# Moving the count of target edges from a graph kernel's second sort into its first, and both spreads of node terms to the start of the second

## The reference

```python
xl = x @ W_lin + b_lin
s_i = xl @ W_att[:hc]
s_j = xl @ W_att[hc:]
alpha = s_i[row] + s_j[col] + b_att
alpha = jnp.where(alpha >= 0, alpha, 0.2 * alpha)
amax = jax.ops.segment_max(alpha, row, num_segments=n)
alpha = jnp.exp(alpha - amax[row])
asum = jax.ops.segment_sum(alpha, row, num_segments=n)
alpha = alpha / (asum[row] + 1e-16)
xh = xl.reshape(n, H, C)
msg = alpha[:, :, None] * xh[row]
out = jax.ops.segment_sum(msg, col, num_segments=n)
```

## Time and profile before

| what | value |
| --- | --- |
| runs | 7012.77, 7015.36 and 7035.64 us |
| the profiled execution | its span is 8156.2 us; no other time of it is given |
| GpSimd busy | 5142.3 us, 63% |
| VectorE busy | 4030.1 us, 49% |
| first sort, block `sa` | 0 to 352 us of the span |
| second sort, block `sd` | 352.6 to 1737 us |
| source softmax, block `st` | 1737 to 1913 us |

### The profile page before, as it was taken

The page is one execution under the profiler, slowest core; times in us unless marked ns, Lnnn a source line. Parts: engine busy times, 40 slices in busy tenths (PEclk is TensorE's granted clock), DMA queues, the critical chain, the costliest instruction groups (busy, mean ns, idle before and its releaser), DMA issues. The chain is left out here.

```text
span 8156.2 us, 28050 instructions
## 1 busy us (share of the span) xinstructions
PE 1077.7 (13%) x4502; PEld 708.5 (9%) x4502; DVE 4030.1 (49%) x8039; ACT 763.0 (9%) x1695; POOL 5142.3 (63%) x4956
## 2 busy tenths in 40 slices
PE   6301022440000000000005565000000001000000
PEld 5200012430000000000003222000000001000000
DVE  8970259673444333333324666667533334336445
ACT  0020012220000000000003333000000003000002
POOL 0277720227777766777764666666777775767774
PEclk9999997775555555555557888555555555555555
DMA  2250000022433333333323677432433331324332
GB/s 49 108 223 2 2 1 0 9 49 63 105 97 97 97 85 101 100 93 93 93 75 118 245 250 252 126 105 70 112 95 93 93 95 44 82 82 122 97 103 60
DMA packets 556796, 772.01 MB, mean 95 GB/s; under 512 B 122155, under 2 KB 433249, under 8 KB 537033
## 3 DMA queue, kind: packets, MB, share of 16 engines
q0 software_dynamic: 159120, 283.64, 14.5%
q1 hardware_dynamic: 379284, 375.57, 14.5%
q10 hardware_dynamic: 18210, 111.02, 3.5%
HBM read 357.68 MB, written 412.16 MB: 94 GB/s over the span
## 5 line engine op out<-in xcount | busy, mean ns | idle before, releaser
L2475 POOL DMA_INDIRECT l2s_krow<-table_k,l2s_idx x784 | 780.9, 996 | 410.5 <-issue 245.8
L929 POOL DMA_INDIRECT l2z_rows<-proj,l2z_idx x784 | 848.6, 1082 | 255.2 <-issue 242.7
L929 POOL DMA_INDIRECT l1z_rows<-table,l1z_idx x784 | 823.4, 1050 | 282.1 <-issue 249.2
L929 POOL DMA_INDIRECT l0z_rows<-table,l0z_idx x784 | 832.3, 1062 | 257.6 <-issue 247.2
L778 POOL DMA_INDIRECT l3z_rows<-table,l3z_idx x784 | 806.0, 1028 | 273.9 <-issue 237.8
L1918 POOL DMA_INDIRECT first_sj<-scores,first_atdst x544 | 559.1, 1028 | 182.2 <-issue 182.2
L2412 DVE SCALAR_TENSOR_TENSOR l2s_qrow<-l2s_qrow,g_dokeep,l2s_zrow 128x82 f32<-128x82 f32 x1568 | 369.3, 300 | 200.6 <-DVE l2s_qrow L2412 138.7
L2430 PE MATMUL l2s_bank<-l2o_wr,l2s_fed 128*128 128x512 f32 x800 | 415.9, 680 | 296.0 <-ACT l2s_fed L2454 171.7
L962 DVE TENSOR_TENSOR l1z_msg<-l1z_rows,l1z_factors 128x1024 f32<-128x1024 f32 (+1 forms) x50 | 60.0, 1200 | 647.4 <-DMA l1z_rows<-table,l1z_idx 633.3
L754 DVE SCALAR_TENSOR_TENSOR l3z_acc<-l3z_acc,l3z_xx,l3z_msg 128x128 f32<-128x128 f32 x784 | 277.8, 354 | 171.8 <-DVE l3z_acc L754 91.5
L962 DVE TENSOR_TENSOR l2z_msg<-l2z_rows,l2z_factors 128x1024 f32<-128x1024 f32 (+1 forms) x50 | 60.0, 1200 | 599.6 <-DMA l2z_rows<-proj,l2z_idx 599.2
(11 more groups left out here) (583 smaller groups left out, 5129.6 us busy)
## 6 DMA issues: line engine op xcount, KB each, us to landing
proj<-l2s_proj ACTq DMA_DIRECT2D x100, 1024.0 KB
spread_q<-prep_zero SPq DMA_DIRECT2D x98, 656.0 KB
l2s_zrow<-spread_q SPq DMA_DIRECT2D x98, 656.0 KB
prefix<-l0z_acc SPq DMA_DIRECT2D x196, 256.0 KB
prefix<-l1z_acc SPq DMA_DIRECT2D x196, 256.0 KB
prefix<-l2z_acc SPq DMA_DIRECT2D x196, 256.0 KB
prefix<-l3z_acc SPq DMA_DIRECT2D x48, 1040.0 KB
l0z_rows<-table,l0z_idx POOLq DMA_INDIRECT x784
```

The lines of the kernel that those rows point to most:

```text
L929: nc.gpsimd.indirect_dma_start(out=rows[:, k % RING, c * (hi - lo) + u, :], out_offset=None, in_=table, in_offset=bass.IndirectOffsetOnAxi ...
L2475: nc.gpsimd.indirect_dma_start(out=krow[:, h, u, :], out_offset=None, in_=g.table_k, in_offset=bass.IndirectOffsetOnAxis(ap=idx[:, h, u:u ...
```

## The change

Four things are moved, and nothing is computed that was not computed before. (1) Both tallies are in the first sort: at each of its 14 turns VectorE offers the batches of the sources and then those of the targets, each kind with a ring of its own, and TensorE counts them in the same order. (2) The positions and node rows of both directions are computed at the end of the first sort, between the last count and the wait for the sorted keys. (3) GpSimd begins the second block with both spreads, 100 indirect DMAs, and fetches the 544 columns of scores behind them; the wait on `placed` is gone, and so is the spread in `st`. (4) The turns of the second sort hold transposes and copies alone.

```diff
--- before.py
+++ after.py
@@ -360,7 +360,7 @@
     chain(v.tensor_scalar(key, key, sign, None, ALU.mult))
 
 
-def sort_by_source(nc, g, a, wide, keys, rows, sjn, raw, count_src, src_s, at_dst):
+def sort_by_source(nc, g, a, wide, keys, rows, sjn, raw, counts, starts, orders, src_s, at_dst):
@@ -382,7 +382,10 @@
         cleared, zeroed, counted = s.sem("cleared"), s.sem("zeroed"), s.sem("counted")
         fkey = s.sb("fkey", [P, NC])
         hi, lo = s.sb("hi", [P, NC]), s.sb("lo", [P, NC])
-        tally = Tally(nc, s, g, "s", raw[:, 0], net.turns)
+        tallies = [Tally(nc, s, g, "st"[k], raw[:, k], net.turns) for k in range(2)]
+        off = s.ps("off", [P, 2])
+        pos = [Positions(nc, s, g, f"p{k}", counts[k], starts[k], off[:, k:k + 1]) for k in range(2)]
+        nid_i, nid, numbered = s.sb("nidi", [P, NB], I32), s.sb("nid", [P, NB]), s.sem("numbered")
         ready, io, vs, filled = s.sem("ready"), s.sem("io"), s.sem("vs"), s.sem("filled")
         edges, plain, nodes, weights, other, padded = (s.sem(n) for n in ("edges", "plain", "nodes", "weights", "other", "padded"))
         set_up, w_ready, b_ready, scored = s.sem("setup"), s.sem("wready"), s.sem("bready"), s.sem("scored")
@@ -399,6 +402,7 @@
                 nc.gpsimd.memset(g.x[96:P], 0.0).then_inc(cleared, 1)
                 pool.wait_ge(cleared, 1)
                 nc.gpsimd.iota(isteps[:], pattern=[[1, P], [0, TALLY]], base=0, channel_multiplier=0).then_inc(io, 1)
+                nc.gpsimd.iota(nid_i[:], pattern=[[1, NB]], base=EP, channel_multiplier=NB).then_inc(numbered, 1)
 
             @block.vector
             def _(eng):
@@ -429,13 +433,21 @@
                         v.memset(g.eps[:], 1e-5)
                         eng.wait_ge(io, 3)
                         chain(v.tensor_copy(g.steps[:], isteps[:]))
+                        eng.wait_ge(numbered, 1)
+                        chain(v.tensor_copy(nid[:], nid_i[:]))
                         eng.wait_ge(plain, 16 * 6)
-                        tally.digits(chain, fkey[:], hi[:], lo[:])
-                    tally.offer(eng, t)
+                        for k in range(2):
+                            tallies[k].digits(chain, fkey[:], hi[:], lo[:])
+                    for k in range(2):
+                        tallies[k].offer(eng, t)
 
                 net.on_vector(eng, later)
-                tally.take(eng, count_src).then_inc(counted, 1)
-                eng.wait_ge(counted, 1)
+                for k in range(2):
+                    tallies[k].take(eng, counts[k]).then_inc(counted, 1)
+                eng.wait_ge(counted, 2)
+                for k in range(2):
+                    pos[k].on_vector(eng, chain)
+                    node_rows(nc, s, f"e{k}", orders[k], chain, counts[k], starts[k], nid[:], k == 1)()
                 eng.wait_ge(fetched, 16)
                 chain(v.tensor_scalar(at_dst, back[:], (1 << MID) - 1, None, ALU.bitwise_and))
                 chain(v.tensor_scalar(back[:], back[:], HIGH, None, ALU.logical_shift_right))
@@ -477,9 +489,12 @@
                 def count(t_):
                     if t_ == 0:
                         pe.wait_ge(zeroed, 1)
-                    tally.count(pe, t_)
+                    for k in range(2):
+                        tallies[k].count(pe, t_)
 
                 net.on_tensor(pe, count)
+                for k in range(2):
+                    pos[k].on_tensor(pe)
 
             @block.scalar
             def _(act):
@@ -565,7 +580,7 @@
                                      in_=rows[:, b, D + k * HEADS:D + (k + 1) * HEADS], in_offset=None).then_inc(sent, 16)
 
 
-def sort_by_target(nc, g, a, wide, keys, pay, raw, counts, starts, at_dst, sjn, sj, got, rows, orders, sent):
+def sort_by_target(nc, g, wide, keys, pay, at_dst, sjn, sj, got, rows, orders, sent):
@@ -579,19 +594,13 @@
         vs, ready, kept, fetched, filled = (s.sem(n) for n in ("vs", "ready", "kept", "fetched", "filled"))
         fkey = s.sb("fkey", [P, NC])
         hi, lo = s.sb("hi", [P, NC]), s.sb("lo", [P, NC])
-        off = s.ps("off", [P, 2])
-        pos = [Positions(nc, s, g, f"p{k}", counts[k], starts[k], off[:, k:k + 1]) for k in range(2)]
-        nid_i, nid = s.sb("nidi", [P, NB], I32), s.sb("nid", [P, NB])
-        tally = Tally(nc, s, g, "t", raw[:, 1], net.turns)
         look = LookUp(nc, s, g, net, at_dst, sjn, sj, fkey[:], hi[:], lo[:], tmp[:].bitcast(F32))
-        counted, numbered, placed = s.sem("counted"), s.sem("numbered"), s.sem("placed")
         with s.block() as block:
             @block.gpsimd
             def _(pool):
-                nc.gpsimd.iota(nid_i[:], pattern=[[1, NB]], base=EP, channel_multiplier=NB).then_inc(numbered, 1)
+                spread_terms(nc, g.spread_s, orders[0], rows, 0, sent[0])
+                spread_terms(nc, g.spread_0, orders[1], rows, 1, sent[1])
                 fetch_columns(nc, g, at_dst, sj, got)
-                pool.wait_ge(placed, 1)
-                spread_terms(nc, g.spread_s, orders[0], rows, 0, sent[0])
 
             @block.vector
             def _(eng):
@@ -606,20 +615,7 @@
                 chain(v.tensor_tensor(wide[:, 0, :], wide[:, 0, :], tmp[:], ALU.bitwise_or))
                 pack(v, chain, keys[0][:], wide[:, 1, :], wide[:, 0, :], tmp[:], g.signs[:, 0:1])
 
-                def tally_on(t):
-                    if t == 0:
-                        tally.digits(chain, fkey[:], hi[:], lo[:])
-                    tally.offer(eng, t)
-
-                net.on_vector(eng, tally_on)
-                tally.take(eng, counts[1]).then_inc(counted, 1)
-                eng.wait_ge(numbered, 1)
-                chain(v.tensor_copy(nid[:], nid_i[:]))
-                eng.wait_ge(counted, 1)
-                for k in range(2):
-                    pos[k].on_vector(eng, chain)
-                    node_rows(nc, s, f"e{k}", orders[k], chain, counts[k], starts[k], nid[:], k == 1)()
-                    eng.sem_inc(placed, 1)
+                net.on_vector(eng, lambda t: None)
                 look.digits(chain)
                 eng.wait_ge(fetched, 16 * 2)
                 chain(v.tensor_scalar(part[:], back[:], (1 << MID) - 1, None, ALU.bitwise_and))
@@ -632,9 +628,7 @@
 
             @block.tensor
             def _(pe):
-                net.on_tensor(pe, lambda t: tally.count(pe, t))
-                for k in range(2):
-                    pos[k].on_tensor(pe)
+                net.on_tensor(pe, lambda t: None)
                 look.on_tensor(pe)
 
             @block.scalar
@@ -2102,7 +2096,6 @@
                 for k, table in enumerate((g.scores_i, g.scores0)):
                     nc.gpsimd.indirect_dma_start(out=init[:, k], out_offset=None, in_=table,
                                                  in_offset=bass.IndirectOffsetOnAxis(ap=firsts[:, k:k + 1], axis=0)).then_inc(started[k], 16)
-                spread_terms(nc, g.spread_0, O.dst, rows, 1, sent[1])
                 pool.wait_ge(stored, 16 * len(chunks))
                 carry.on_pool(pool)
                 for k, group in enumerate(GROUPS):
@@ -2552,9 +2545,9 @@
                 keys = [q.sb(f"key{h}", [P, WIDE]) for h in range(2)]
                 pay = [wide[:, 3, :].bitcast(F32), q.sb("pay1", [P, WIDE])]
                 raw = q.sb("raw", [P, 2, NC], I32)
-                sort_by_source(nc, g, a, wide, keys, rows, sjn[:], raw, count_src[:], src_s[:], at_dst[:])
-                sort_by_target(nc, g, a, wide, keys, pay, raw, (count_src[:], count_dst[:]), (start_src[:], start_dst[:]),
-                               at_dst, sjn[:], sj, got, rows, orders, sent)
+                sort_by_source(nc, g, a, wide, keys, rows, sjn[:], raw, (count_src[:], count_dst[:]), (start_src[:], start_dst[:]),
+                               orders, src_s[:], at_dst[:])
+                sort_by_target(nc, g, wide, keys, pay, at_dst, sjn[:], sj, got, rows, orders, sent)
             with Space(nc, "mid") as q:
                 sj_d = q.sb("sjd", [P, HEADS, NC])
                 source_softmax(nc, g, O, rows, sj, got, src_s, orders[0], sent, sj_d)
```

## The result

The changed kernel takes 7095.63 us (median of 5 runs, 7092.91 to 7144.96) against 7021.79 us (5 runs, 7012.77 to 7035.64) for the kernel before on the same chip: 1.012 times as long, 95% interval 1.01 to 1.014. The medians are 74 us apart, and the ratio, which takes all runs in, stands for 84; the forecast sum was 82. What the sum was made of came out less well, as the blocks show.

The account below looks back on a forecast made before the run. VectorE was taken to bound the second block before the change, GpSimd after it. The terms +88, 0, +2, -2 and -6 summed to +82 us, 7097 us; the 8-in-10 range was 7015 to 7140, the likeliest case alone 7054 to 7145.

Parts of the forecast that it names:

- +88 + 2 - 2 - 6 = +82: Sum in us: more tally in the first sort +88, its positions +2, second block -2, third block -6.
- The strange recording: Profile of the kernel before: 335.1 us of unnamed waits in the second sort, taken as a price of recording.
- the gap of 1140.8 us: Profiled span of 8156.2 us against the runs' median of 7015.36; some 1110 us of it was accounted for.
- First sort, +88: 49 added batches in the first sort at TensorE's 1.79 us each: +88 us, bounds 80 to 98.
- Second sort on VectorE, -82: Batches and digits leave, payload waits appear, look-up starts earlier: VectorE's end in the second block goes from 838 to 754 us.
- exposed payload waits: Second sort: VectorE waits about 1.45 us at an across turn and 0.7 at a back turn; seven pairs, 15 us.
- GpSimd in the second block: It becomes the bound: stream of 835 us, block 836 instead of 838, so -2; bounds -30 to +31.
- VectorE bounds the block with 67 us to spare: Second block of the kernel before, undisturbed: VectorE ends at 838 us, GpSimd at 771.
- The scans, -6: Third block: the target spread leaves, so stores and the table load can go earlier; -6 us, bounds -2 to -13.
- GpSimd does not bind: Rival, second block: a fetch takes under 1.15 us, VectorE still ends the block; about 0, 7015 us; chance 0.12.
- The stall is real: Rival, second sort: the unnamed waits exist in the runs too; -12 us in all, about 7000; chance 0.13.
- TensorE's clock: Rival, look-up: granted clock 0.50 adds 126 us to VectorE's chain, +45 in all, 7142 us; chance 0.05.

Follow-up runs that it names:

- kernel before again: The kernel before, unedited, run and recorded once more: 7023.79 us, ratio 0.9996 to before.
- counts alone: The changed kernel with GpSimd's order of fetches and spreads as in the kernel before: 7095.18 us, ratio 1.0095 to before.
- changed kernel again: The changed kernel, unedited, run and recorded once more: 7097.95 us, ratio 1.0116 to before.
- spreads behind: The changed kernel with GpSimd's two spreads put behind its 544 fetches: 7135.93 us, ratio 1.0158 to before.

## Why the prediction was right, and where it was not

**The sum.** Forecast +88 + 2 - 2 - 6 = +82. By the blocks of the two new recordings: +87.1 (both tally terms), +23.5, -20.5, so +90; by the runs +74 to +84. The direction and the main term stand on a right mechanism: the batches cost VectorE their full price in the first sort, where nothing hides them, and in the second sort GpSimd ends the block. But the total is as close as it is by luck, because two errors had opposite signs: the second sort came out 25 us above its term, the scans 14 below theirs.

**The strange recording.** Right: the waits of the earlier trace rows and the gap of 1140.8 us are not in the runs; the kernel before has a span of 7024.1 when recorded again. Wrong in part is what I made of it. I called it the price of recording GpSimd's stream, and had the changed kernel's profile show it again only if the stall were real. As twelve further recordings have no such stretch, it is no price of recording as such, but belongs to one execution. No run of any kernel here comes near that length either. The Trainium skill's page "NOTIFIC — the notification-queue block" (section 7.1) says that the block that writes trace records holds its producers back rather than lose one inside. That is neither shown nor refuted here: no run shows what the stall was. My own account of the gap was rough too. The second block is 537 us shorter in the new recording (1385 and 848), where I had 546. But from their first DMA to their last the five gathers fell by 449 us in all (5505 and 5056), where I had 565, and some 146 lay in stages that the account left out. I had taken 1.25 us as the rate of every undisturbed gather, and `l2s` needs 1.32 ((779.3+257.3)/784) in the kernel before again:

```profile
L2475 POOL DMA_INDIRECT l2s_krow<-table_k,l2s_idx x784 | 779.3, 994 | 261.4 <-issue 257.3
```

**First sort, +88.** The size is right (83.7 for the batches). Which engine sets it was not: I had TensorE as the slower one at 1.79 us a batch, with VectorE's waits to grow to 15 to 25 us. The two waits sum to 9.5, where they were 9.2, and the increase is VectorE's own 59.8 + 27.9 = 87.7 us. Both ways gave 88, which is luck of the two prices.

**Second sort on VectorE, -82.** 840 to 761 us, -79; the exposed payload waits are 7.4 + 7.0 = 14.4 us against 15 forecast. The heading's 82 is a slip: the working gives 78 + 6 = 84, from 838 to 754, and the sum used the 754. So this term came out 5 us too large, and its mechanism holds.

**GpSimd in the second block.** Here is the step that was wrong though the total came out right: "VectorE bounds the block with 67 us to spare". It had none; both engines ended at 840. The term is 544 fetches at 1.30 us, 707. They took 775 (1.425 each). By the table of pauses, 47 of the missing 68 are the periods over 2.7 us, and the rest small ones. I had taken 1.28 us from an undisturbed stretch of 39 DMAs and put away the whole stretch's 1.363 as distorted by the recording, when it was the better guide and still too low. For the changed stream I had 128 + 707 = 835; recorded again it is 142 + 724 = 866, so 31 more, which is the far end of the range I gave; in the first recording it was 886, and the block 892, beyond that range. As GpSimd already set the end before, the 80 us that VectorE saves showed as 18 even with nothing else moved (counts alone), and the 50 added DMAs turn that into a loss of 23.5.

The small losses depend on what VectorE does beside the fetches. These are stretches of the changed kernel again, fetches alone (busy, count, clock, DMA share, GB/s): beside the sort, beside the look-up, and when VectorE was idle.

```profile
590.00:990.00 400.00, 305.16 (x292) 0.69 0.12 27
1010.00:1190.00 180.00, 134.27 (x141) 0.99 0.06 3
1210.00:1300.00 90.00, 65.75 (x71) 0.50 0.06 2
```

400/292 is 1.37 us a fetch, pauses included, 180/141 is 1.28, and 90/71 is 1.27; without the periods over 2.7 us they are 1.31, 1.26 and 1.25, and 1.36 beside the sort with its tally (560 to 980 us in the kernel before again). So it is not VectorE's being busy that slows GpSimd: in the look-up VectorE was busy for 177 of 191 us. Where the fetches stand first, the small losses are 49, 48, 45 and 44 us with the tally on VectorE beside them, and 32 and 30 without it (counts alone, spreads behind). Two recordings of the changed kernel differ by 11 in this, so I take it that the moved tally gave GpSimd some 15 us, on the evidence of single recordings. The page "DMA: Bandwidth & Descriptors" of the Trainium skill (section "SWDGE vs HWDGE vs iDMA") says that GpSimd writes its descriptors into state in SBUF that VectorE locks it out of while it runs in its 2-port performance mode. The traces agree in that some work of VectorE slows GpSimd and other work does not; which instructions run in that mode they do not show, and which of them does it was not tried.

**The scans, -6.** It is -20.5. I had the mechanism (SyncE's stores held by the load that waits for the spread) but assumed that two thirds of the profile's 19.3 us go and half of that is missing in the runs. Recorded again, `st_crow` was 18.9 us late before, and is 4.0 late now, not the 8 to 10 of the forecast: so 15 go, and 1 in front of the scans and 4 behind `st_crow` go as well. The discount for a recording effect was an error: the waits here were real.

**Rivals.** "GpSimd does not bind" is out, since fewer fetches help the changed kernel at once and hurt the one before. "The stall is real": out by the recordings. "TensorE's clock": the granted clock is 0.99 in the look-up (1.00 before), so the engine is at its upper level, 2.4 GHz, and VectorE waits 0.9 us for it in all:

```profile
1009.00:1200.00 191.00, 154.70 (x928) 132.09 (x928) 177.18 (x271) 80.32 (x114) 142.77 (x150) 0.99 0.06 3
```

## What to carry to other kernels

Before believing a profile, set its span against the time of the runs; where they differ by more than the runs do among themselves, take another recording, for a stretch that looks distorted can also hide which engine is the true bound. Work that is taken from one of two engines that end together is worth little until the other one is relieved as well (80 us off VectorE gave 18 here); ask first by how much the second is behind, with its rate over the whole block and not over its best stretch. And work moved to a place where nothing else runs costs its full price there: here 49 batches that hid for the most part beside a GpSimd stream came to stand alone, for 84 us.

## What was not expected of the hardware

- One execution of the same program was 1132 us longer than another (8156.2 and 7024.1), with unnamed waits spread over it; none of twelve further recorded executions had it.
- GpSimd's stream of indirect DMAs has pauses, up to single instructions of 18 to 28 us in a row of 0.95 us ones, and they are bound to places in the program: a period of 4.0 to 5.0 us at the 113th and the 226th fetch of each group in every kernel, 8.1 to 8.4 where 98 transfers of 656 KB (400 GB/s) run beside it, and the longer ones within three DMAs behind such a place, but not in every execution.
- The period of such a DMA, pauses included, is 1.27 us beside an idle VectorE, 1.28 beside its look-up and 1.37 beside its sort. A scatter of 128 rows costs 1.27 us at the end of the block and 1.42 to 1.53 at its start, there with and without the transfers beside it.
